# Layer 1 self-attention: probabilities normalised on GpSimd, values as the stationary operand

## The reference, cut to what matters

```
q = einsum('bsd,dhk->bshk', x, Wq) + bq      # x is layer-normed; h = 16, k = 64
k = einsum('bsd,dhk->bshk', x, Wk) + bk
v = einsum('bsd,dhk->bshk', x, Wv) + bv
attn = softmax(einsum('bqhk,bshk->bhqs', q, k) / sqrt(64), axis=-1)
ctx = einsum('bhqs,bshk->bqhk', attn, v)
y = x + einsum('bqhk,hkd->bqd', ctx, Wo) + bo
return (y - mean(y)) * rsqrt(var(y) + 0.001) * gamma + beta
```

## Time and profile before

| | |
|---|---|
| time, median of 3 runs | 1788.22 us (1783.66 to 1791.61) |
| the profiled execution | 1790.74 us |
| its span | 1789.0 us |
| PE, PEld busy in the span | 1257.9 us (70%), 834.9 us (47%) |
| DVE, ACT, POOL busy | 1175.0 us (66%), 768.9 us (43%), 155.2 us (9%) |
| phase L1a, from its first keys to the last update of `X` | 468.7 us to 759.7 us |
| its loop of 32 units, from the first scores in it to the last `project` | 502.8 us to 753.1 us |

### The profile page before, as it was taken

One profiled execution on the slowest core, in us unless ns is written; L12 is line 12 of the kernel. 1 busy time (PEld: TensorE's weight loads), 2 busy tenths in 40 slices (PEclk: granted clock), 3 DMA queues, 4 the chain that ended last, 5 costly groups with the idle time before them and its releaser, 6 DMA issues.

```text
span 1789.0 us, 25090 instructions
## 1 busy us (share of the span) xinstructions
PE 1257.9 (70%) x8858; PEld 834.9 (47%) x8870; DVE 1175.0 (66%) x2883; ACT 768.9 (43%) x1410; POOL 155.2 (9%) x132
## 2 busy tenths in 40 slices
PE   5998889954799999799933798987889700001665
PEld 2555555533478878745522454554554400001444
DVE  2654557877556676487767576885764389994446
ACT  1544346754355445346645433664434314430221
POOL 2210103100000000012011001110000000000001
PEclk7888789987899999889966776999999955555678
DMA  3000300000000000000000000000002300001000
GB/s 116 13 13 13 138 7 7 7 1 0 1 1 1 1 1 7 7 7 7 7 1 0 1 1 7 13 1 1 0 0 55 79 19 0 0 1 53 18 0 23
DMA packets 28805, 28.11 MB, mean 16 GB/s; under 512 B 12192, under 2 KB 23456, under 8 KB 27808
## 3 DMA queue, kind: packets, MB, share of 16 engines
q1 hardware_dynamic: 28704, 26.76, 4.9%
HBM read 20.20 MB, written 6.55 MB: 15 GB/s over the span
## 4 chain that ended last, share of the span: by engine, by line
PE 46%; issue 21%; DVE 21%; ACT 8%; DVEq 2%; POOL 2%; DMA 1%; SPq 1%; POOLq 0%; ACTq 0%
PE PSA L842 3%; PE PSA L995 3%; PE PSA L832 3%; PE PSA L1280 2%; PE PSA L682 2%; DVE BIG L2474 2%; PE PSA L688 2%; PE PSA L665 2%; PE PSA L1012 2%; PE PSA L975 2%; PE PSA L949 2%; ACT BIG L1483 2%; PE PSA L961 2%; PE PSA L956 2%; DVE BIG L2466 2%
## 5 line engine op out<-in xcount | busy, mean ns | idle before, releaser
L1307 PE MATMUL PSA<-W,TMP 128*128 128x128 f32 x32 | 8.3, 441 | 215.2 <-DVE TMP L2496 215.2
L1490 ACT ACTIVATE QK<-PSA 128x512 f32<-128x512 f32 x192 | 104.7, 595 | 110.3 <-PE PSA L842 110.3
L528 POOL TENSOR_TENSOR RSTD<-VEPS,HALF 128x4 f32<-128x4 f32 x50 | 50.7, 1015 | 947.3 <-DVE VEPS L1801 947.3
L1920 DVE TENSOR_TENSOR BIG<-PSA,MX 128x1024 f32<-128x1024 f32 x96 | 117.5, 1224 | 12.3 <-PE PSA L842 9.3
L832 PE MATMUL PSA<-BIG 32*128 32x512 f32 x384 | 114.3, 685 | 15.0 <-DVE BIG L1920 13.9
L1916 DVE TENSOR_REDUCE MX<-PSA 128x8 f32<-128x1024 f32 x96 | 116.8, 1216 | 6.2 <-PE PSA L832 5.6
L1483 ACT ACTIVATE BIG<-BIG 128x1024 f32<-128x1024 f32 x96 | 101.7, 1059 | 25.2 <-DVE BIG L1920 25.2
L842 PE MATMUL PSA<-K,BIG 128*128 128x128 f32 x768 | 107.0, 285 | 6.4 <-ACT BIG L1483 4.8
L842 PEld LDWEIGHTS PSA<-K,BIG 128*128 128x128 f32 x768 | 90.8, 146 | 40.1 <-ACT BIG L1483 28.1
L1307 PEld LDWEIGHTS PSA<-W,TMP 128*128 128x128 f32 x32 | 7.1, 327 | 216.4 <-DVE TMP L2496 216.4
L534 POOL TENSOR_SCALAR BIG<-BIG,COLS 128x512 f32<-128x512 f32 x52 | 80.5, 1564 | 261.1 <-ACT BIG L1475 140.4
(11 more groups left out here) (373 smaller groups left out, 3059.7 us busy)
## 6 DMA issues: line engine op xcount, KB each, us to landing
CTX<-in_ctx_t SPq DMA_DIRECT2D x16, 256.0 KB, 3.1
W<-in_w SPq DMA_DIRECT2D x1, 2048.0 KB, 7.2
W<-in_w SPq DMA_DIRECT2D x1, 1412.0 KB, 11.8
ROWS<-in_rows SPq DMA_DIRECT2D x1, 1232.0 KB, 8.9
scratch_q<-TMP SPq DMA_DIRECT2D x4, 256.0 KB, 2.0
W<-scratch_q SPq DMA_DIRECT2D x64, 16.0 KB
W<-in_w SPq DMA_DIRECT2D x2, 512.0 KB, 10.7
scratch_q<-BIG SPq DMA_DIRECT2D x4, 256.0 KB, 2.3
```

The source lines that it names most:

```text
L528: pool.tensor_tensor(RSTD[:, 0, :], VEPS[:, 0, :], HALF[:], ALU.pow).then_inc(ln_rstd.sem, 1)
L1490: act.activation(PT[:, m % 2, c, :], PS[4 + c], ACT.Copy).then_inc(p_ready.sem, 1)
L1920: dve.tensor_tensor(tile(PH[:, m % 2, :], 8), s, last(high, P), ALU.subtract).then_inc(shifted.sem, 1)
```

## The change: what it does

The exponentials are normalised before they are transposed. DVE adds them up in SBUF (`inverse_sum`, L2012 of the new file) and inverts the sums (L2014); POOL multiplies the 1024 columns of the unit by them (L564). `PH1` gets four buffers, and the scores run four units ahead, not three. The column of ones goes, and with it POOL's write of it and `normalise` on DVE.

The values become the stationary operand, 64 columns of a head, and the transposed probabilities the moving one (128 columns). Even heads write partitions 0 to 63 of bank 5, odd heads 64 to 127, so two heads stand on the two column halves of the array, and all eight heads of a unit fill bank 5 once. The outputs come out transposed as `project` wants them; the transposes back go, and ACT copies bank 5 straight to `OT1`. DVE no longer touches bank 5.

```
-        V1 = BIG[:, 8192:12352].rearrange("p (n s h d) -> p n s h d", n=2, s=2, h=H)
-        PH1 = BIG[:, 12352:14400].rearrange("p (n t) -> p n t", n=2)
-        ON1 = QK[:, 4:8, :].rearrange("p (n a) t -> p n (a t)", n=2)
+        V1 = BIG[:, 8192:12288].rearrange("p (n s h d) -> p n s h d", n=2, s=2, h=H)
+        PH1 = [BIG[:, 12288:13312], BIG[:, 13312:14336]] + [QK[:, 4 + 2 * n:6 + 2 * n, :]... for n in range(2)]
...
 # POOL
-                    pool.memset(V1[:, :, :, :, 64:65], 1.0).then_inc(setup_pool, 1)
                     ln_root(p, 0)
-                    for it in range(GROUPS - 1):
-                        ln_root(p, it + 1)
-                        root(p, it, 0)
+                    for m in range(GROUPS * HALVES):
+                        it, e = m // HALVES, m % HALVES
+                        if e == 3 and it:
+                            root(p, it - 1, 0)
+                        if e == 1 and it:
+                            ln_root(p, it)
+                        pool.wait_ge(inverse_ready.sem, inverse_ready.at(p, 0, m))
+                        pool.tensor_tensor(tile(PH1[m % 4], 8), tile(PH1[m % 4], 8), last(RD[:, 8 * (m % 4):8 * (m % 4) + 8], P), ALU.mult
+                                           ).then_inc(scaled.sem, 1)
...
 # PE, transposes
-                        pe.wait_ge(exp_ready.sem, exp_ready.at(p, 0, m))
+                        pe.wait_ge(scaled.sem, scaled.at(p, 0, m))
...
-                def product(m, r):
+                def product(m):
                     pair, s, h = m // 4, m % 4 // 2, m % 2
...
                     for x in range(4):
-                        mm = pe.matmul(dst[:, x * 65:(x + 1) * 65], PT[:, m % 2, r, tok(x)], V1[:, pair % 2, s, 8 * h + 2 * x + r, :],
-                                       start=True, stop=True)
+                        for r in range(2):
+                            mm = pe.matmul(dst[64 * r:64 * r + 64, tok(x)], V1[:, pair % 2, s, 8 * h + 2 * x + r, :], PT[:, m % 2, r, tok(x)],
+                                           start=True, stop=True)
                     mm.then_inc(pv_done.sem, 1)
-                    freed[5] = on_ready, on_ready.at(p, 0, 2 * m + r)
-
-                def outputs(n, half, b):
...
+                    freed[5] = ot_ready, ot_ready.at(p, 0, m)
...
 # ACT
-                def outputs(n, half, b):
-                    act.wait_ge(ot_psum.sem, ot_psum.at(p, 0, 2 * n + half))
-                    act.activation(OT1[:, 4 * half:4 * half + 4, :], tile(PS[b]), ACT.Copy).then_inc(ot_ready.sem, 1)
+                def outputs(m):
+                    act.wait_ge(pv_done.sem, pv_done.at(p, 0, m))
+                    if m >= 2 and m % 2 == 0:
+                        act.wait_ge(y_psum.sem, y_psum.at(p, 0, m // 2 - 1))
+                    act.activation(OT1[:, 4 * (m % 2):4 * (m % 2) + 4, :], tile(PS[5]), ACT.Copy).then_inc(ot_ready.sem, 1)
...
 # DVE
-                def normalise(m, r):
...
+                def inverse_sum(m):
+                    rd = RD[:, 8 * (m % 4):8 * (m % 4) + 8]
+                    total_of = SS1[:, m % 2, :]
+                    dve.wait_ge(exp_ready.sem, exp_ready.at(p, 0, m))
+                    dve.tensor_reduce(total_of, tile(PH1[m % 4], 8), AX_X, ALU.add).then_inc(sum_taken.sem, 1)
+                    dve.wait_ge(sum_taken.sem, sum_taken.at(p, 0, m))
+                    dve.reciprocal(rd, total_of).then_inc(inverse_ready.sem, 1)
...
                 shift(2)
-                dve.drain()
+                inverse_sum(0)
                 next_normed(p, 0)
+                take_max(3)
+                shift(3)
+                inverse_sum(1)
                 for m in range(total):
...
-                    if m + 3 < total:
-                        take_max(m + 3)
-                    normalise(m, 0)
+                    if m + 4 < total:
+                        take_max(m + 4)
+                        shift(m + 4)
...
-                    if m + 3 < total:
-                        shift(m + 3)
-                    normalise(m, 1)
+                    if m + 2 < total:
+                        inverse_sum(m + 2)
```

More of the change, by code:

```diff
@@ L198, in decoder @@
         Q1 = BIG[:, 4096:8192].rearrange("p (n c t) -> p n c t", n=2, c=8)
-        V1 = BIG[:, 8192:12352].rearrange("p (n s h d) -> p n s h d", n=2, s=2, h=H)
-        PH1 = BIG[:, 12352:14400].rearrange("p (n t) -> p n t", n=2)
+        V1 = BIG[:, 8192:12288].rearrange("p (n s h d) -> p n s h d", n=2, s=2, h=H)
+        PH1 = [BIG[:, 12288:13312], BIG[:, 13312:14336]] + [QK[:, 4 + 2 * n:6 + 2 * n, :].rearrange("p a t -> p (a t)") for n in range(2)]
         OT1 = BIG[:, 14400:15424].rearrange("p (c t) -> p c t", c=8)
         BVB = BIG[:, 14400:15424].rearrange("p (c t) -> p c t", c=8)
-        ON1 = QK[:, 4:8, :].rearrange("p (n a) t -> p n (a t)", n=2)
         KN = BIG[:, 0:1024].rearrange("p (n t) -> p n t", n=2)
@@ L334, in decoder @@
         t_psum = signal("t_psum", quarters)
+        sum_taken = signal("sum_taken", {"L1a": HALVES})
+        inverse_ready = signal("inverse_ready", {"L1a": HALVES})
+        scaled = signal("scaled", {"L1a": HALVES})
         s2_psum = signal("s2_psum", {"L2a": GB * 2})
         p_ready = signal("p_ready", {**quarters, "L2a": GB * 2})
[L337 to L340, removed]
+        pv_done = signal("pv_done", {**units, "L2a": GB})
+        on_ready = signal("on_ready", cross(GB))
+        ot_psum = signal("ot_psum", each(("L0a", "L1x", "L2x")))
+        ot_ready = signal("ot_ready", {**each(("L0a", "L1x", "L2x", "L2a")), "L1a": HALVES})
         y_psum = signal("y_psum", {**each([p for p in PHASES if p not in ("scan", "L3a", "L0x")]), "L1a": GB})
@@ L1040, in l1_attention @@
                 values(1, 1, 7)
+                scores(2)
+                scores(3)
                 transposes(0, 0)
-                scores(2)
                 transposes(0, 1)
@@ L1047, in l1_attention @@
                     done, first, second = m >= 2 and m % 2 == 0, pair + 1 < total // 4, pair + 2 < total // 4
-                    if m + 3 < total:
[L1049 to L1052, removed]
+                    if m + 4 < total:
+                        scores(m + 4)
                     if q == 0 and first:
@@ L1062, in l1_attention @@
                         queries(pair + 2, 3, 7)
+                    if m + 1 < total:
+                        transposes(m + 1, 0)
+                    product(m)
                     if done:
-                        outputs(n, 0, 7)
-                    if m + 1 < total:
-                        transposes(m + 1, 1)
+                        project(n, 6)
                     if q == 1 and second:
@@ L1070, in l1_attention @@
                         values(pair + 2, 0, 6)
-                    if done:
-                        outputs(n, 1, 6)
-                    product(m, 1)
+                    if m + 1 < total:
+                        transposes(m + 1, 1)
                     if q == 0 and first:
@@ L1572, in l1_attention @@
                 values(1, 1, 7)
-                exp(0)
-                copy(0, 0)
-                exp(1)
-                copy(0, 1)
-                exp(2)
+                for m in range(3):
+                    exp(m)
+                for r in range(2):
+                    copy(0, r)
                 for m in range(total):
-                    pair, q, n = m // 4, m % 4, m // 2 - 1
-                    done, first, second = m >= 2 and m % 2 == 0, pair + 1 < total // 4, pair + 2 < total // 4
-                    if m + 1 < total:
-                        copy(m + 1, 0)
+                    pair, q = m // 4, m % 4
+                    first, second = pair + 1 < total // 4, pair + 2 < total // 4
                     if q == 0 and first:
@@ L1590, in l1_attention @@
                         keys(pair + 2, 3, 6)
-                    if done:
-                        outputs(n, 0, 7)
                     if m + 1 < total:
-                        copy(m + 1, 1)
+                        copy(m + 1, 0)
+                    outputs(m)
                     if q == 1 and second:
@@ L1598, in l1_attention @@
                         values(pair + 2, 0, 6)
-                    if done:
-                        outputs(n, 1, 6)
+                    if m + 1 < total:
+                        copy(m + 1, 1)
                     if q == 0 and first:
```

47 lines of the change are left out of this document (11 added, 36 removed).

## The result

| | before | after |
|---|---|---|
| median of the runs, us | 1787.89 (1783.66 to 1791.61, 4 runs) | 1761.59 (1759.32 to 1762.98, 4 runs) |
| the profiled execution, its span, us | 1790.74, 1789.0 | 1762.98, 1761.2 |
| phase L1a, first keys to the last update of `X`, us | 290.9 | 266.6 |

The ratio is 0.9852, 95% interval 0.9827 to 0.9877: 26.3 us less, where 20 were forecast (1768, range 1752 to 1790). A later measurement of both kernels gave the same ratio, 0.9852 (0.9833 to 0.9871).

What follows compares the result with a forecast made beforehand. PE was taken to bound the first three groups. Groups and entry summed as -5.8 - 5.4 - 3.7 - 10.2 + 5.5 = -19.6 us, from 1790.7 to 1771; with the median 2.5 us lower, 1768, range 1752 to 1790.

Steps and rivals of the forecast that it cites:

- PE's chain: Middle of a group: PE bounds from end to end; products take 1.27 us a unit, a pair 28.1 instead of 31.6.
- the four strips: Cross-attention's products, 16 passes on four column strips in 0.56 us, taken as 1.12 us on two strips.
- The transposes back: PE's transposes of the outputs, 0.44 + 0.47 us a sequence, go in 16 sequences: 14.6 us less on PE.
- POOL's multiplication: Normalising 1024 columns on POOL each unit: 3.1 us, just hidden in steady units, where up to 4.3 us are hidden.
- Holds of DVE: Three places a group where POOL's instruction holds DVE: next_normed, keep_input, end of post_stats; up to 3.1, 1.6, 2.2 us.
- Second and third group: Loop groups with an update: 5 us of stall behind it, 62.0 us each in place of 67.4 and 65.7.
- Fourth group: Last group of the loop, keys and queries run out: 44.2 us in place of 54.4, including 4 us of stall.
- Entry: Start of the loop: 2.9 us lost before it, with the second transposes' wait 5.5 us together.
- Halves in turn: Rival for PE's products: the array's halves take turns, 0.66 us more a unit, 1789 us; chance 0.08.
- POOL's bound: Rival: POOL's multiplication takes 6.2 us and bounds the kernel, 27 us more, 1815 us; chance 0.11.
- DVE's queue: Rival: DVE's queue never recovers, PE waits some 2 us a pair for banks 6 and 7, 1781 us; chance 0.12.
- A larger gain: Rival: products at 0.89 us, POOL's multiplication at 2 us or less with short holds, 1750 us; chance 0.14.

Runs made afterwards that it cites:

- e2: The changed kernel with the second row of transposes of every unit made twice, four more transposes a unit; 1772.10 us.
- e1: The changed kernel with a unit's products reordered, first the four even heads, then the four odd ones, not alternating; 1772.71 us.
- e7: The kernel before the change with only one of the four transposes back in each row of them; 1786.21 us.
- e4: The changed kernel with POOL's multiplication run three times, the first two into a spare tile; 1837.54 us.
- e3: The changed kernel with a second POOL multiplication of the same size, into a spare buffer, ahead of each; 1794.5 us.
- e5: The changed kernel without POOL's multiplication, the probabilities left unnormalised and PE's transposes waiting for DVE's inverse; 1755.37 us.
- e6: The changed kernel with DVE's queue reordered: attention's result taken before the query bias, update of X in four parts, input kept later; 1767.4 us.
- e9: e6 with ACT's exponentials and DVE's update reordered in the last group, and POOL's multiplication in two separately released halves; 1753.61 us.
- e11: e9 with PE transposing the identity 32 times at the entry while it waits for POOL; 1747.6 us.

## Why the prediction was right, point by point

The phase was forecast 19.6 us shorter and is 24.3 shorter, with errors that in part offset each other: the entry came out 1.6 us better, the second and third group 7.0, the fourth 3.9 worse. So that the number came so near is partly luck.

**PE's chain.** Right. PE bounds the middle of the loop (e2), and the products' halves overlap (e1). I took 1.27 us a product. It is 1.02 and the projection behind it, every second unit, is longer by 0.20: 1.12 a unit. So the 1.12 from the four strips held, and the 0.15 on top of it was too much: 0.6 us a pair, which came in 0.5 under the 28.1.

**The transposes back.** Right in the change (they go, with the wait in front of them), though e7 shows that shortening them alone would have paid half.

**POOL's multiplication.** Mis-sized, with two errors that offset each other. It takes 1.90 us; I took 3.1, from a row with another operation. And I set too low what 3.1 us would have cost. The loop around POOL needs 10.9 us in the units with biases, where I had 10.7 (9.7 and two biases of 0.48): 3.1 would have made 14.0 of 13.8, so "just fits" was a little off. A straight line between the measured points at 1.90 and 3.8 us, an estimate, gives a ratio of 0.996 at 3.1, 1781 us in place of my 1768, and no gain from 3.5 us on (I said 4.4). The next step, to 5.7 us, costs more than this one (e4), so the true cost at 3.1 may lie below the line. That the forecast held rests on the price being lower than I thought.

The Trainium skill (GPSIMD Engine Reference, Elementwise — side-by-side cycle accounting) was nearer with 2.25 us, an estimate from its figure for an addition of 2048 columns. The traces have 1.90 us, and 1.86 from one start to the next (537.13 to 538.99 in e3).

**Holds of DVE.** Right in kind, smaller in size. `next_normed` was held four times, and `post_update` in the fourth: 2.36 us for three instructions, where in e5 all four of them take 1.06. `keep_input` stayed at 0.69, since POOL had finished. By the Trainium skill (SBUF — State Buffer, Who interferes with whom) `keep_input`, with two inputs from SBUF, is to wait when POOL reads there, and the sum never; the traces agree with both, 2.39 us for `keep_input` in e3 and 1.17 to 1.22 for the sum in all runs.

**Second and third group.** The stall behind the update was forecast at 5 us. It is one wait of 1.8 us in each, and e6 gave back 2.0 (56.5 against 58.5). It was built on a POOL of 3.1 us and on three holds that come late in the queue, of which one showed. That the second group gained 1.7 us more than the third is the clock of the kernel before: its second group ran at 0.97, with a product at 1.08 us behind the update's wait, and runs at 1.00 now.

**Fourth group.** The step that came out worst on the other side: 48.1 us against 44.2. I let PE set its pace. It is a chain over ACT, DVE and POOL in which PE waits for POOL's 1.9 us, and PE's clock falls behind some of these waits. e5 takes POOL away and gives 7.0 us, with PE busy for 32.9 us at a clock of 1.00 in place of 37.2 at 0.89; e9 gives 5.0 by halves alone.

**Entry.** 3.9 against 5.5, but the two do not measure the same. My 5.5 was 4.1 us to the loop's first scores, less 1.24 for the row of scores ahead of them, plus 2.6 for a wait of the second unit's transposes, which would lie in the first group. The 44.2 us of the fourth group hold one row of scores less already, so the 1.24 was taken off twice. As the table measures it, the forecast was +4.1 for the entry, -3.2 for the first group and -18.4 in all. The wait of 2.6 us did not show: in the first group PE idles for 0.7 us, for ACT. And 4.1 us with POOL at 3.1 would be 2.9 at 1.90; the measured 3.9 has the lower clock in it, of which e11 gave back 1.0 here and 1.0 in the first group. POOL's own part is 2.0 us (e5).

**The rivals.** Halves in turn: excluded by e1. POOL's bound: the mechanism is real and close, as e3 shows with twice the price. DVE's queue: it recovers; PE waits once behind the update in the second and in the third group, and the pair that follows lasts 27.6 us again. A larger gain: its price of POOL came true (1.90 us), its product in part (1.02, and 0.20 on the projection), and the second and third group were 7.0 us better than forecast; the fourth group took 3.9 of that back.

What stays open is why the clock in a later phase rises sooner in some kernels' executions, with the same code there. And no run takes the fourth unit of scores ahead, with its two more buffers `PH1`, apart from the rest of the change; the middle pairs leave little for it, since the rows that PE lost and gained make up their 4.0 us.

## What to carry to other kernels

Where a step goes to another engine, work out the whole loop of hand-overs it closes, with everything that stands ahead in each queue, and compare its slack with the uncertainty of the price: here the slack was 1.0 us and my error on the price 1.2. Here the price of the new operation hid in the steady loop and came due where there was no other work to cover it, at the entry and in the last group; there, release the result in parts and keep the queue in the order of need. And before a wait in the chain is counted as a loss, look at whether the engine idled.

## What the runs showed of the hardware beyond that

- 16 passes with 64 columns of weights take 1.02 us when the two halves of the array alternate, 1.51 in turn; 16 full passes took 1.78.
- POOL's product of two float32 tensors, one of them a value per head repeated, takes 1.90 us for 1024 columns, and two of 512 take 2.04 (1.04 each, the second starting a little before the first ends), so by estimate about 0.14 us of it are fixed.
- PE's clock costs where it waits: behind 4.18 us of idling at the entry 16 passes of scores took 2.08 us at a granted clock of 0.50 (e9), and 1.16 at 1.00 with PE kept at work on spare transposes (e11). But the same wait of 1.78 us was followed by the lower clock in e5's third group and not in the changed kernel's.
